# A graph-network kernel on one core: one scatter semaphore per column tile, edge test first, self-loop term and small root chains on GpSimd

## The reference, cut to what matters

```python
# layer 0
adj1 = adj + eye;  degree = adj1.sum(axis=2)
d = degree ** -0.5;  d = where(isinf(d), 0, d)
x = layernorm(x + (d[:, :, None] * adj1 * d[:, None, :]) @ (x @ W0) + b0)
# layer 1
m_j = x @ W1[:D];  m_i = x @ W1[D:]
pre[b,i,j,:] = m_j[b,j,:] + m_i[b,i,:] + b1
msg = gelu(layernorm(pre, g1, be1))              # exact gelu
agg[b,i,:] = sum over j of msg[b,i,j,:] * adj[b,i,j]
out = layernorm(x + layernorm(concat(x, agg) @ W2 + b2, g2, be2))
```

## Time and profile before

| | us |
|---|---|
| median of 3 executions (4471.06 to 4480.56) | 4475.62 |
| the profiled execution's own time | 4462.46 |
| its span | 4460.7 |
| busy: TensorE (PE) | 4053.9 (91%) |
| busy: weight loads (PEld) | 3315.2 (74%) |
| busy: ScalarE (ACT) | 3499.8 (78%) |
| busy: VectorE (DVE) | 3204.8 (72%) |
| busy: GpSimd (POOL) | 1271.1 (28%) |

### The profile page before, as it was taken

The page is one execution under the profiler, slowest core; times in us unless marked ns, Lnnn a source line. Parts: engine busy times, 40 slices in busy tenths (PEclk is TensorE's granted clock), DMA queues, the critical chain, the costliest instruction groups (busy, mean ns, idle before and its releaser), DMA issues.

```text
span 4460.7 us, 97279 instructions
## 1 busy us (share of the span) xinstructions
PE 4053.9 (91%) x30654; PEld 3315.2 (74%) x30655; DVE 3204.8 (72%) x8038; ACT 3499.8 (78%) x9481; POOL 1271.1 (28%) x1041
## 2 busy tenths in 40 slices
PE   3899899998989989999999999989999999999998
PEld 2677777777767777777777777777777777777777
DVE  3677677777767776777777767767777777778777
ACT  2787787877868778787877878788888888878887
POOL 2222332133312323212333223332123333123320
PEclk8899999999989999999999999999999999999999
DMA  1212221122201222112221112221122221122210
GB/s 47 70 62 77 69 74 40 52 76 77 69 27 59 77 68 77 39 52 74 77 69 54 47 62 77 69 74 41 53 73 77 73 73 55 44 66 77 65 57 14
DMA packets 245646, 276.82 MB, mean 62 GB/s; under 512 B 22320, under 2 KB 204080, under 8 KB 245040
## 3 DMA queue, kind: packets, MB, share of 16 engines
q1 hardware_dynamic: 212272, 168.62, 12.7%
q0 software_dynamic: 32768, 100.70, 6.1%
HBM read 160.17 MB, written 109.05 MB: 60 GB/s over the span
## 4 chain that ended last, share of the span: by engine, by line
PE 61%; issue 12%; POOL 10%; ACT 9%; DVE 4%; DMA 2%; DVEq 0%; POOLq 0%; SPq 0%; ACTq 0%; PEldq 0%
PE z_even_ps L1257 11%; POOL table L427 10%; PE agg_odd_ps L1220 9%; PE z_odd_ps L1257 9%; PE agg_even_ps L1220 8%; PE z_even_ps L1253 3%; PE p_ps L1139 3%; PE z_odd_ps L1253 3%; ACT tmp L618 3%; PE p_ps L1082 2%; PE p_ps L1140 2%; DMA table<-stage,row_id 2%; ACT root L549 1%; ACT msg L605 1%; PE p_ps L1116 1%
## 5 line engine op out<-in xcount | busy, mean ns | idle before, releaser
L618 ACT ACTIVATE tmp<-nbr,r_sb 128x128 f32<-128x128 f32 x4864 | 1519.2, 389 | 29.1
L990 DVE SCALAR_TENSOR_TENSOR pick<-rank,root_p 128x512 f32<-128x512 bf16 (+3 forms) x1664 | 889.6, 553 | 79.3 <-ACT rank L568 79.2
L1020 DVE SCALAR_TENSOR_TENSOR spread<-rankT,nbr 128x512 f32<-128x512 bf16 (+3 forms) x1664 | 907.9, 568 | 0.0
L427 POOL DMA_INDIRECT table<-stage,row_id x512 | 626.6, 1224 | 559.9 <-issue 513.3
L605 ACT ACTIVATE msg<-msg 128x768 f32<-128x768 f32 (+1 forms) x896 | 728.5, 813 | 34.6 <-issue 31.4
L1257 PEld LDWEIGHTS z_even_ps<-mi_g,pick 128*128 128x128 f32 x5120 | 640.2, 200 | 150.2 <-issue 150.2
L1257 PE MATMUL z_even_ps<-mi_g,pick 128*128 128x129 f32 x5120 | 729.4, 294 | 0.0
L1257 PEld LDWEIGHTS z_odd_ps<-mi_g,pick 128*128 128x128 f32 x5120 | 609.0, 192 | 146.6 <-issue 146.6
L1257 PE MATMUL z_odd_ps<-mi_g,pick 128*128 128x129 f32 x5120 | 695.5, 285 | 1.3 <-issue 1.2
L1220 PE MATMUL agg_even_ps<-spread,msg 128*128 128x128 f32 x5120 | 675.6, 283 | 4.5 <-issue 4.5
L1220 PE MATMUL agg_odd_ps<-spread,msg 128*128 128x128 f32 x5120 | 648.5, 276 | 21.7 <-DVE spread L1020 15.7
(11 more groups left out here) (217 smaller groups left out, 5180.8 us busy)
## 6 DMA issues: line engine op xcount, KB each, us to landing
nbr<-table SPq DMA_DIRECT2D x128, 512.0 KB, 3.9
adj_g<-in_adj SPq DMA_DIRECT2D x32, 1024.0 KB, 6.3
nbr_root<-table SPq DMA_DIRECT2D x128, 256.0 KB, 4.6
nbr_heavy<-table SPq DMA_DIRECT2D x512, 32.0 KB, 3.6
x_g<-in_x SPq DMA_DIRECT2D x32, 256.0 KB, 3.2
table<-stage,row_id POOLq DMA_INDIRECT x512
out<-out_sb SPq DMA_DIRECT2D x32, 256.0 KB, 2.3
w_sb<-in_L_gnn_W SPq DMA_DIRECT2D x2, 128.0 KB, 2.2
```

What stands on the lines that cost most here:

```text
L427: pool.indirect_dma_start(table[q], bass.IndirectOffsetOnAxis(ap=row_id[:, jt * TB + it:jt * TB + it + 1], axis=0), stage[:, jt, it, :], N ...
L618: last = act.activation(tmp[:, c % 2, n - FROM[u], :], half_row, ACT.Identity, scale=r_sb[:, c % 2, n - FROM[u]:n - FROM[u] + 1])
L990: ins = dve.scalar_tensor_tensor(into.rearrange("p k n -> p (k n)"), rank[:, it, span], float(MARK + t), root_p[:, it, span], ALU.is_equal ...
L1020: ins = dve.scalar_tensor_tensor(into, rankT[:, it, jt:jt + count, :], float(MARK + t), nbr[:, it, jt:jt + count, 0:P], ALU.is_equal, ALU. ...
```

## The change

- The counter p_scat becomes four, one per column tile jt, with SC = 64 for a graph. ACT waits at each of its four evictions for the scatters of its own tile; GpSimd's copy for m_j does the same. SyncE and DVE wait for all four.
- In DVE's slots `sort` (edge_p) comes ahead of `last_run`, `finish` and `prepare`.
- The four products with the identity (L1083) go. GpSimd instead multiplies sup by d, and adds that to pre_g, in step S_SUP + 1, with the first tile of `half` as the place between; DVE's S_PRE waits for it.
- Each root chain becomes: DVE writes v, GpSimd raises it to the power -0.5 in the step after, DVE uses the result at the slot at which the chain ended before (third slot, two steps after the chain's first). The chain x starts two slots later, with the degree in a tile of its own; where the degree is 0, 1 is put in its place for the power, and the mask `nonzero` gives 0 as before. ACT waits for the third count of p_dis.

```diff
-        SC = TB * TB * 16
+        p_scat = [sem(f"p_scat{jt}") for jt in range(TB)]
+        SC = TB * 16
...
                 if it == 0:
-                    wait_alone(sp, p_scat, (a + 1) * SC)
+                    for jt in range(TB):
+                        wait_alone(sp, p_scat[jt], (a + 1) * SC)
...
+            pool.memset(minus_half[:, :], -0.5).then_inc(s_ident, 1)
...
+            def root_of_x(n, s):
+                if s == S_X + 1:
+                    wait_alone(pool, x_seq, n * POWS + 1)
+                    pool.tensor_tensor(x_y[:, :], x_v[:, :], minus_half[:, :], ALU.pow).then_inc(x_seq, 1)
+
             def prepare(a, q, s):
+                if s == S_Y + 1:
+                    wait_alone(pool, y_seq, a * POWS + 1)
+                    pool.tensor_tensor(y_y[:, :], y_v[:, :], minus_half[:, 0:TB], ALU.pow).then_inc(y_seq, 1)
...
+                if s == S_SUP + 1:
+                    own = half[:, 0, :].rearrange("p (t o) -> p t o", t=TB)
+                    wait_alone(pool, p_ev, a * NF + (F_SUP + 1))
+                    wait_alone(pool, p_dis, a * 2 + 2)
+                    if not is_int(a, 1):
+                        wait_alone(pool, p_mask, a * TB)
+                    pool.tensor_tensor(own, sup[:, :, :], dis[:, :].unsqueeze(2).to_broadcast([P, TB, D]), ALU.mult).then_inc(p_own, 1)
+                    wait_alone(pool, p_own, a * 2 + 1)
+                    wait_alone(pool, p_xb, a + 1)
+                    pool.tensor_tensor(pre_g[:, :, :], pre_g[:, :, :], own, ALU.add).then_inc(p_own, 1)
...
-                    if not is_int(a, 1):
-                        wait_alone(pool, p_scat, a * SC)
                     for jt in range(TB):
+                        if not is_int(a, 1):
+                            wait_alone(pool, p_scat[jt], a * SC)
...
-                                            stage[:, jt, it, :], None).then_inc(p_scat, 16)
+                                            stage[:, jt, it, :], None).then_inc(p_scat[jt], 16)
...
             def finish(e, q, s):
+                if s == Z_RUN + 1:
+                    wait_alone(pool, z_seq, e * POWS + 1)
+                    pool.tensor_tensor(z_y[:, :], z_v[:, :], minus_half[:, 0:TB], ALU.pow).then_inc(z_seq, 1)
...
                 a, s = cx.prepared(i)
+                if i < PC + GC and (a is not None or cx.ended(i) is not None):
+                    root_of_x(cx.b + ((i + AHEAD) // GC + 1), (i + AHEAD) % GC)
                 if a is not None:
                     prepare(a, (i + AHEAD) // GC % 2 ^ 1, s)
...
                     if s == S_AT + jt:
                         filled(F_AT + jt)
-                        if jt == 0 and not is_int(a, 1):
-                            act.wait_ge(p_scat, a * SC)
+                        if not is_int(a, 1):
+                            act.wait_ge(p_scat[jt], a * SC)
...
                 if s == S_SUP:
                     filled(F_SUP)
-                    act.wait_ge(p_dis, a * 2 + 2)
+                    act.wait_ge(p_dis, a * 3 + 3)
...
-                        last = dve.tensor_scalar(x_v[:, 0:TB], deg[:, :], 1.0, None, ALU.add)
+                        dve.tensor_scalar(degree[:, :], deg[:, :], 1.0, None, ALU.add).then_inc(p_dis, 1)
+                if (s, slot) == (S_X, 2):
...
+                    if a is not None:
+                        dve.wait_ge(p_dis, a * 3 + 1)
+                        dve.tensor_scalar(nonzero[:, :], degree[:, :], 0.0, None, ALU.not_equal).then_inc(p_dis, 1)
+                        last = dve.scalar_tensor_tensor(x_v[:, 0:TB], degree[:, :], 0.0, degree[:, :], ALU.is_equal, ALU.add)
...
-                j = (s - S_X) * RUNS + slot - 1
-                if 0 <= j < STEPS:
-                    dve.wait_ge(x_seq, n * (STEPS + 1) + (j + 1))
-                    rsqrt(j, x_v[:, :], x_i[:, :], x_u[:, :], x_y[:, :]).then_inc(x_seq, 1)
...
-                        dve.wait_ge(p_xb, a + 1)
+                        dve.wait_ge(p_own, a * 2 + 2)
...
                 def others(slot):
+                    if k_sort is not None:
+                        sort(cx.tiles + k_sort, t_sort, slot)
...
-                    if k_sort is not None:
-                        sort(cx.tiles + k_sort, t_sort, slot)
...
                         for mt in range(TB):
-                            mm(dst, stage[:, mt, it, 0:P], sup[:, mt, :], start=(mt == 0), stop=False)
-                        last = mm(dst, ident[:, :], sup[:, it, :], start=False, stop=True)
+                            last = mm(dst, stage[:, mt, it, 0:P], sup[:, mt, :], start=(mt == 0), stop=(mt == TB - 1))
```

More of the change, by code:

```diff
@@ L20 @@
 EPS = 1e-5
-MAGIC = float(0x5F3759DF)
-STEPS = 11
+POWS = 2
 CUBE_K = math.sqrt(0.375)
@@ L151, in adj_resnorm_kernel @@
         stage = sb("stage", [P, TB, TB, 3 * P])
-        x_v, x_i, x_u, x_y = (sb(f"x_{n}", [P, 2 * TB], U32 if n == "i" else FP32) for n in "viuy")
-        y_v, y_i, y_u, y_y = (sb(f"y_{n}", [P, TB], U32 if n == "i" else FP32) for n in "viuy")
-        z_v, z_i, z_u, z_y = (sb(f"z_{n}", [P, TB], U32 if n == "i" else FP32) for n in "viuy")
+        x_v, x_y = (sb(f"x_{n}", [P, 2 * TB]) for n in "vy")
+        y_v, y_y = (sb(f"y_{n}", [P, TB]) for n in "vy")
+        z_v, z_y = (sb(f"z_{n}", [P, TB]) for n in "vy")
+        minus_half = sb("minus_half", [P, 2 * TB])
+        degree = sb("degree", [P, TB])
         shift1 = sb("shift1", [P, TB])
@@ L214, in adj_resnorm_kernel @@
         (p_load, p_xb, p_edge, p_deg, p_fill, p_ev, p_hb, p_mask, p_dis, p_pre, p_st1, p_h,
-         p_shift, p_cls, p_place, p_copy, p_scat) = (
+         p_shift, p_cls, p_place, p_copy, p_own) = (
             sem(f"p_{n}") for n in ("load", "xb", "edge", "deg", "fill", "ev", "hb", "mask",
-                                    "dis", "pre", "st1", "h", "shift", "cls", "place", "copy", "scat"))
+                                    "dis", "pre", "st1", "h", "shift", "cls", "place", "copy", "own"))
+        p_scat = [sem(f"p_scat{jt}") for jt in range(TB)]
         p_seed, p_sq, p_new, p_cube, p_left = (sem(f"p_{n}") for n in ("seed", "sq", "new", "cube", "left"))
@@ L233, in adj_resnorm_kernel @@
         N_CONST = 3 + 7 + 1
-        N_IDENT = 13
-        SC = TB * TB * 16
+        N_IDENT = 14
+        SC = TB * 16
         def wait_alone(eng, sem, value):
@@ L460, in alone @@
                 for s in range(GC):
+                    root_of_x(0, s)
                     prepare(0, 0, s)
@@ L463, in alone @@
                 for i in range(AHEAD):
+                    root_of_x(1, i)
                     prepare(1, 1, i)
@@ L487, in prepare @@
                             if not is_int(a, 1):
-                                act.wait_ge(x_seq, a * (STEPS + 1))
+                                act.wait_ge(x_seq, a * POWS)
                                 act.wait_ge(p_fill, a * NF - (NF - F_CNT - 1))
@@ L716, in _ @@
             dve.sem_inc(s_setup, 1)
-            def rsqrt(j, v, ii, uu, y):
-                if j == 0:
-                    return dve.tensor_scalar(ii, v.bitcast(U32), 1, None, ALU.logical_shift_right)
-                if j == 1:
-                    return dve.tensor_scalar(y.bitcast(U32), ii, -1.0, MAGIC, ALU.mult, ALU.add)
-                if j % 3 == 2:
-                    return dve.scalar_tensor_tensor(uu, y, -0.5, y, ALU.mult, ALU.mult)
-                if j % 3 == 0:
-                    return dve.tensor_tensor(uu, uu, v, ALU.mult)
-                return dve.scalar_tensor_tensor(y, uu, 1.5, y, ALU.add, ALU.mult)
             def last_run(a, e, n, s, slot):
@@ L740, in last_run @@
                         last = dve.tensor_scalar(x_v[:, TB:2 * TB], mv3[:, :, 1], EPS, None, ALU.add)
+                    if a is not None:
+                        dve.wait_ge(p_dis, a * 3 + 1)
+                        dve.tensor_scalar(nonzero[:, :], degree[:, :], 0.0, None, ALU.not_equal).then_inc(p_dis, 1)
+                        last = dve.scalar_tensor_tensor(x_v[:, 0:TB], degree[:, :], 0.0, degree[:, :], ALU.is_equal, ALU.add)
                     last.then_inc(x_seq, 1)
-                j = (s - S_X) * RUNS + slot - 1
-                if 0 <= j < STEPS:
-                    dve.wait_ge(x_seq, n * (STEPS + 1) + (j + 1))
-                    rsqrt(j, x_v[:, :], x_i[:, :], x_u[:, :], x_y[:, :]).then_inc(x_seq, 1)
-                if a is not None and j == STEPS - 3:
-                    dve.wait_ge(x_seq, a * (STEPS + 1) + 1)
-                    dve.tensor_scalar(nonzero[:, :], x_v[:, 0:TB], 0.0, None, ALU.not_equal).then_inc(p_dis, 1)
-                if j == STEPS:
-                    dve.wait_ge(x_seq, (n + 1) * (STEPS + 1))
+                if (s, slot) == (S_X + 2, 2):
+                    dve.wait_ge(x_seq, (n + 1) * POWS)
                     if a is not None:
-                        dve.wait_ge(p_dis, a * 2 + 1)
+                        dve.wait_ge(p_dis, a * 3 + 2)
                         dve.tensor_tensor(dis[:, :], x_y[:, 0:TB], nonzero[:, :], ALU.mult).then_inc(p_dis, 1)
```

(3 more changed lines are left out.)

18 lines of the change are left out of this document (5 added, 13 removed).

## The result

| | before | after |
|---|---|---|
| median, us | 4475.35 (4 runs, 4471.06 to 4480.56) | 4369.9 (4 runs, 4359.83 to 4372.22) |
| ratio, 95% interval | | 0.9756 [0.9742, 0.977] |
| profiled execution; span | 4462.46; 4460.7 | 4369.12; 4367.4 |
| granted clock, mean | 0.961 | 0.960 |

The forecast was 4371. The unaltered kernel ran in two more comparisons, both on one chip (which chip the first ran on isn't recorded): there it took 4554.4 and 4550.7 us, 1.0179 and 1.0191 of before. So the text has two subjects: where the 105 us of the first comparison came from, and why the same program is 181 to 185 us longer in the two others.

The account below looks back on a forecast made before the run. ACT's first eviction waits for all 16 scatters, 5.4 us a graph. Semaphores 2.3 + identity's product 0.9 + root chains 0.2 = 3.4 us a graph, x 31 = 105 us: median 4475.6 to 4371, range 4290 to 4450.

Parts of the forecast that it names:

- the next wait: TensorE's transposes (L1152): with ACT's stall gone, they wait for the table's read, 1 to 5 us in most graphs.
- edge_p's wait: TensorE's wait for edge_p (1.6 us each, 30 times) shrinks by 1.2 us, costed at 0.
- 2.3 x 31 = 71: Scatter semaphores per column tile: mean gain of 2.3 us a graph, from 1.9 in long graphs and 2.9 in short ones.
- the identity's product: Four products a graph leave TensorE, 0.22 us each: 0.9 us a graph gained.
- GpSimd's additions holding DVE: Two GpSimd additions might slow DVE by 1.1 us each, 2.2 us a graph; taken as 0.
- the three powers block too: By the lock rule GpSimd's powers also hold DVE; on a critical DVE the change would keep 1.2 us, not 3.4.
- 0.6 x 3.8 + 0.4 x 2.9 = 3.4 us earlier: TensorE's first table transpose (L1152) comes 3.8 us earlier in long graphs, 2.9 in short ones, before the clock's price.
- rival (a): The read hardly binds: scatters keep pace, the clock stays up; 6.0 us a graph gained, 4290 us; chance 12%.
- The first step that failed: GpSimd's scatters: with DVE busy, four more gaps take 1.75 instead of 1.33 us, delaying the read's data by 1.7 us.
- 0.6 x 1.9 = 1.1 lost to the clock: Behind L1152 the lower clock costs 1.9 us in long graphs (bounds 0 and 3.2); short graphs wait too briefly for it.
- Forecast 0.6 us with an upper bound of 1.27: GpSimd's x power takes 0.6 us, hidden; nearest rows 0.16 and 1.27 us; room for some 3.4 us.
- Rival (d): GpSimd's x power is a long routine, making dis late and ACT stand; at 10 us 4575 us; chance 9%.

Follow-up runs that it names:

- e1: The kernel before with the four scatter semaphores alone; 4383.27 us, 0.9854 of before.
- e8: The changed kernel with the identity products back on TensorE and without GpSimd's two additions; 4580.52 us, 1.0241 of before.
- e6: The changed kernel with 128 semaphore increments at the head of TensorE's program, to shift its instructions; 4573.51 us, 1.0232 of before.
- e3: The changed kernel with TensorE's transposes waiting for the light read (nbr) alone, not nbr_heavy; 4432.0 us, 0.9983 of before.
- e2: The changed kernel with ACT waiting for all 16 scatters at its first eviction again; 4571.95 us, 1.0296 of before.
- e4: The changed kernel with GpSimd's edge step two steps later (S_EDGE = 4); 4589.51 us, 1.0341 of before.
- e5: The changed kernel, unaltered, in a later comparison on a second chip; 4554.4 us, 1.0179 of before.
- e10: The kernel before with the powers on GpSimd in place of the root chains, and nothing else of the change; 4577.15 us, 1.0259 of before.
- e7: The changed kernel with the three root chains back on DVE; 4379.24 us, 0.9772 of before.
- e11: The changed kernel with its root chains back on DVE, run a second time; 4385.64 us, 0.9808 of before.
- e12: The changed kernel with root chains back on DVE and TensorE's table transposes waiting for the light read alone; 4385.93 us, 0.9823 of before.

## Why the prediction was right, and where it wasn't

**Right by its own steps, in the first comparison.** ACT's stall went; the read became the next wait, in 28 of 31 graphs of the whole change; the clock fell behind it; edge_p's wait shrank by 1.1 us (forecast 1.2) without a gain of its own that shows; DVE was seldom last. e1 gives the semaphores 65 us where 2.3 x 31 = 71 had been forecast, though not by the forecast's way: the read hardly binds there. e8 gives the identity's product 0.84 us a graph (forecast 0.9), though both of its sides hold the late dispatch. Of GpSimd's additions holding DVE nothing shows: in the graph above they run from 2137.72 to 2140.30, while DVE waits 3.18 us for ACT until 2140.49. The rule of the Trainium skill, SBUF — State Buffer, "Who interferes with whom", would hold a DVE operation with two SBUF inputs back there, and in this graph none asks. In the whole span eight spreads of 128x512 run partly beside L408, none over 0.69 us.

The prediction drew from that rule that the three powers block too. The trace doesn't agree: of 70 picks and spreads of 128x512 that ran beside a power (8 beside x's, 31 each beside y's and z's) none took over 0.70 us, as alone. What was slowed, and what the forecast didn't have, are those beside the edge test (L417): 130 of 163 took about 1.09 us in place of 0.68, where before none of 91 did. That is some 53 us of DVE's time; as TensorE's waits for DVE stay small, no run shows that it cost anything.

**Two terms mis-sized, in opposite senses.** The forecast had TensorE's transpose 0.6 x 3.8 + 0.4 x 2.9 = 3.4 us earlier, with scatters slipping by 1.7 us; measured 4.9 us, which is what rival (a) had. The scatters took 23.9 us and not 25.0. The first step that failed is the one that took 1.75 us between scatters, in place of 1.33, as the price of a busy DVE for four more of them. After the change ACT doesn't stand there and DVE is busy for 3.48 of 5.21 us (before, 3.48 of 6.65), and the last four intervals are still 1.30 us on average (2114.09 to 2119.30). The mean of 1.75 us held the one long scatter of the row, 3.04 us; without it it is 1.57.

The second is the clock. For the rest of the graph the forecast had 0 (1.1 gained, 0.6 x 1.9 = 1.1 lost to the clock, as the drop was to come in 6 of 10 graphs only); measured is 1.6 us lost. The drop came in 29 of 30 graphs, mostly behind waits of 2.9 us, which the forecast had taken as too short for it; the trace of before had it, for 3 us or more, in 28 of 30 graphs already. In the graph shown, 3.4 us at 1.2 GHz follow on an idle time of 2.94 us, and in before's, 6.8 us on 5.00. By an estimate from these rows, the clock took 2.7 us if the 1.1 us came in full, and 5.7 us more at half the clock would cost up to 2.8. The sum is 3.2 us a graph against 3.4. So the close hit, 4369.9 for 4371, is in part luck: the two errors cancel.

**The powers.** Forecast 0.6 us with an upper bound of 1.27. Over the span (ns min/median/max):

```profile
L391 POOL TENSOR_TENSOR x_y<-x_v,minus_half x35: 1647/1676/2459, 51.2 to 4357.6; 128x8 f32<-128x8 f32 x35
...
L396 POOL TENSOR_TENSOR y_y<-y_v,minus_half x32: 1025/1290/1293, 63.1 to 4121.0; 128x4 f32<-128x4 f32 x32
```

So the bound from the additions was too low: a power of 8 columns takes 1.68 us, more than an addition of 512. Under the 3.4 us at which it would have mattered, it delays DVE's dis in 28 graphs, by 8.6 us in the lone first graph and by 0.6 us on average in the others, where about 1 had been forecast. ACT's sup stood for dis only in the first two graphs, 14.1 us in all. z's power, of 4 columns too, has a median of 1.75 us.

**What it missed.** Rival (d) had the x power turn the change into a loss by being a long routine, at 10 us. The loss that came in the other comparisons goes with the same instructions and is not that: the power takes 1.7 us there too. Before's profile has a little of it, 5.9 us of such gaps, all but 0.2 of them while scatters run, which the prediction didn't use. It looked at GpSimd's busy time and its users, not at whether the three other engines would be handed their instructions in time.

**Open.** Why three small GpSimd operations more a graph, and 33 small DVE ones less, bring the late dispatch on one chip and not in the first comparison. Whether it is the powers themselves or the missing DVE chains isn't settled, as no kernel had powers on DVE or the chains beside the powers. A third reading is open too: each of these edits moves the instructions of GpSimd, DVE and ACT within their programs, and e6 moved TensorE's alone. That e3 takes nearly all of the late graphs away by another wait speaks for a matter of timing or place rather than of the powers as such; no run tells these apart. Whether the chip decides or something else of the session isn't either; e2 and e4 show the late dispatch on the first of the two chips, e5, e6 and e8 to e10 on the second.

**The version to keep.** e7/e11, the change without the powers: 0.9772 and 0.9808 where the whole change gives 1.0179 and 1.0191. It beats before in both comparisons. It was not run beside a whole change that gains, so against the 0.9756 of the first comparison it may give up some 0.2 to 0.5%.

## What to carry to other kernels

When a wait for a transfer goes, price the next user of the same transfer: here a stall of 5.4 us a graph on one engine came back as one of 3.5 us (97.7 / 28) on another. Judge a change on more than one chip or hour before keeping it, and where engines stand with "issue" or "remote" in the middle of a group that waits for nothing, look at what else runs in that window before looking at the instructions themselves. A small operation moved to an idle engine isn't free merely because it is short: take each such move as an edit of its own, with a run of its own.

## What the runs showed that was not expected

- The same program took 4370 us in one comparison and 4551 to 4554 in two others, with 0.2 against 96 to 114 us of gaps in TensorE's groups of products.
- TensorE, ACT and DVE fall short together while a row of 16 indirect scatters runs, and the 16 scatters take 21.1 us then, against 23 to 29 us otherwise.
- GpSimd's power costs 1.29 us (y) or 1.75 us (z) for 128x4 and 1.68 us for 128x8 (medians), as much as 512 columns of an addition (1.27 us) or more.
- With the wait for the heavy read taken from TensorE (e3, e12), it stood for "issue" up to 5 us in 26 graphs ahead of the next transposes; the ratio didn't move from e11 to e12.
- The clock fell behind an idle time of 2.9 us too, in 29 of 30 graphs. The time at 1.2 GHz moved with the wait and didn't shrink (352 us before, 355 after).
- DVE's picks and spreads of 128x512 took 1.09 us in place of 0.68 beside GpSimd's edge test in the changed kernel (130 of 163), and never before (0 of 91); beside the powers none was slowed.
